# Layer 0 of the style convolutions: the second tap's high and low data stacked in one matmul

## The reference

```python
def _layer(x, style, w, b, mw, mb, typ):
    s = style @ mw.T + mb
    weight = SCALE * w * s[:, None, :, None]
    demod = lax.rsqrt(jnp.sum(weight * weight, axis=(2, 3)) + EPS)
    weight = weight * demod[:, :, None, None]
    ...
# TYPES = ('same', 'upsample', 'same', 'downsample')
x = x + _L0_ffn_ref(_L0_cond_ref(x, cond_512, ...), ...)
# _L0_ffn_ref: cw = top-4 weights of sigmoid(x @ gate_w.T) + bias
#   out = sum_e (silu(x @ Wg[e].T) * (x @ Wu[e].T) * cw[:, e]) @ Wd[e].T
#   out += silu(x @ Sg.T) * (x @ Su.T) @ Sd.T
```

## Time and profile before

| | us |
|---|---|
| three runs, median | 1182.87 |
| three runs, lowest and highest | 1182.38, 1185.62 |
| profiled execution, its own time | 1183.04 |
| its span (first to last instruction) | 1181.3 |
| PE busy | 1121.3 |
| DVE busy | 797.0 |
| ACT busy | 516.6 |
| POOL busy | 539.8 |

### The profile page before, as it was taken

The page is one execution under the profiler, slowest core; times in us unless marked ns, Lnnn a source line. Parts: engine busy times, 40 slices in busy tenths (PEclk is TensorE's granted clock), DMA queues, the critical chain, the costliest instruction groups (busy, mean ns, idle before and its releaser), DMA issues. The chain is left out here.

```text
span 1181.3 us, 24581 instructions
## 1 busy us (share of the span) xinstructions
PE 1121.3 (95%) x7149; PEld 1006.2 (85%) x7150; DVE 797.0 (67%) x2043; ACT 516.6 (44%) x1245; POOL 539.8 (46%) x639
## 2 busy tenths in 40 slices
PE   4999999999999977979999999999999999999995
PEld 2788888888888866769999999999998899999995
DVE  7788887888888875745655656556567565555653
ACT  4776666666666663122322323223234232222321
POOL 1000131323222364555656565665655566656663
PEclk7999999999999987989999999999999999999998
DMA  7855666666556542267676666766676676665664
GB/s 240 205 144 152 150 151 154 157 154 152 143 143 161 143 100 54 77 176 161 128 149 119 155 118 112 162 114 156 125 160 152 150 174 113 114 112 109 116 115 71
DMA packets 140254, 163.64 MB, mean 139 GB/s; under 512 B 31456, under 2 KB 97088, under 8 KB 138688
## 3 DMA queue, kind: packets, MB, share of 16 engines
q0 software_dynamic: 36000, 75.39, 34.0%
q1 hardware_dynamic: 103888, 87.58, 27.6%
q10 hardware_dynamic: 336, 0.32, 0.1%
HBM read 74.58 MB, written 55.18 MB: 110 GB/s over the span
## 5 line engine op out<-in xcount | busy, mean ns | idle before, releaser
L437 POOL DMA_INDIRECT lists<-entry,place x128 | 127.2, 994 | 347.6 <-DVE x_lo L778 285.8
L1426 PE MATMUL bank<-xt_hi,wup_hi 128*128 128x256 f32 x1104 | 278.2, 284 | 2.0 <-ACT xt_hi L694 1.5
L1426 PE MATMUL bank<-xt_hi,wup_lo 128*128 128x256 f32 x1104 | 278.0, 284 | 0.0
L493 POOL DMA_INDIRECT out_rows<-placed,sid x140 | 227.2, 1623 | 92.4 <-DVE placed L1153 69.2
L581 ACT ACTIVATE t<-bank,cB,cA 128x256 f32<-128x256 f32 (+1 forms) x384 | 176.6, 536 | 102.4 <-PE bank L230 96.7
L1426 PEld LDWEIGHTS bank<-xt_hi,wup_hi 128*128 128x128 f32 x1104 | 212.4, 192 | 6.6 <-issue 2.1
L1426 PEld LDWEIGHTS bank<-xt_hi,wup_lo 128*128 128x128 f32 x1104 | 212.7, 193 | 2.4
L478 POOL DMA_INDIRECT placed<-h_rows,gid x140 | 141.6, 1012 | 119.0 <-PE bank L1404 80.3
L1430 PE MATMUL bank<-xt_lo,wup_hi 128*128 128x256 f32 x1104 | 178.0, 284 | 0.0
L711 ACT ACTIVATE zt_hi<-z 128x256 fp32r<-128x256 f32 x138 | 57.6, 417 | 228.9 <-DVE z L1143 228.9
L1153 DVE TENSOR_SCALAR placed<-bank,all_lists 128x512 f32<-128x512 f32 x138 | 99.6, 748 | 83.4 <-DMA out_rows<-placed,sid 46.1
(11 more groups left out here) (258 smaller groups left out, 2085.4 us busy)
## 6 DMA issues: line engine op xcount, KB each, us to landing
x<-x1p SPq DMA_DIRECT2D x64, 384.0 KB
wraw<-in_Wup SPq DMA_DIRECT2D x11, 1024.0 KB, 7.6
xraw<-in_xq SPq DMA_DIRECT2D x32, 260.0 KB, 2.8
xbase<-in_x SPq DMA_DIRECT2D x32, 256.0 KB, 2.8
h_rows<-hrow SPq DMA_DIRECT2D x128, 64.0 KB
x<-x1p SPq DMA_DIRECT2D x64, 127.0 KB
out_rows<-orow SPq DMA_DIRECT2D x30, 256.0 KB, 2.0
wdraw<-in_Wdn SPq DMA_DIRECT2D x11, 512.0 KB, 10.1
```

What stands on the lines that cost most here:

```text
L437: pool.indirect_dma_start(out=lists, out_offset=bass.IndirectOffsetOnAxis(ap=place[:, home, r, k:k + 1], axis=0), in_=entry[:, home, r, k, ...
L493: pool.indirect_dma_start(out=out, out_offset=bass.IndirectOffsetOnAxis(ap=sid[:, u:u + 1], axis=0), in_=yb[:, u, :], in_offset=None, comp ...
L1426: pe.matmul(dst, lhs[a], rhs[0], start=k == 0 and a == 0, stop=False)
```

## The change

Layer 0's second tap reads only 64 partitions, those of q = 0 and q = 1. The change makes a new tile x0n in which the high part of these 64 partitions stands on partitions 0 to 63 and the low part on 64 to 127, put there by two DMAs (`stack_next`), and repeats the entries of these 64 rows on the other 64 in the second tap's matrix. One matmul with the high weights then does high by high and high by low of that tap; one with 64 rows does low by high. Block 0 still does all six matmuls, its second tap on 64 partitions. For the others there are five, and the last waits for both copies.

```diff
+        x0n = sb("x0n", [P, NB, VP], F32R)
...
+            def stack_next(g):
+                sp.wait_ge(S["x0_hi"], g + 1)
+                sp.wait_ge(S["x0_lo"], g + 1)
+                for a in range(2):
+                    sp.dma_start(x0n[a * (P // 2):(a + 1) * (P // 2)].rearrange("p b v -> p (b v)").bitcast(F32),
+                                 x0[a][0:P // 2].rearrange("p b v -> p (b v)").bitcast(F32)).then_inc(S["x0_stacked"], 16)
+
             stack(0)
             sp.wait_ge(S["x0_hi"], 1)
             sp.wait_ge(S["x0_lo"], 1)
             sp.dma_start(xraw[:, 0], xq[2]).then_inc(S["x_loaded0"], 16)
+            stack_next(1)
...
                     sp.dma_start(xraw[:, 1 - odd], xq[bass.ds(g + 3, 1)].rearrange("a p b v -> p (a b) v")).then_inc(S[f"x_loaded{1 - odd}"], 16)
+                if within(g, 0, G - 2):
+                    stack_next(g + 2)
...
-                same = [columns(FIRST + m, P, lambda a: x0[a][:, :, m:m + V]) for m in range(2)]
+                here = columns(FIRST, P, lambda a: x0[a][:, :, 0:V])
+                following = columns(FIRST + 1, P // 2, lambda a: x0[a][0:P // 2, :, 1:V + 1])
                 pe.wait_ge(S["x0_hi"], g + 1)
-                hi_passes(pe, dst, same)
-                pe.wait_ge(S["x0_lo"], g + 1)
-                lo_passes(pe, dst, same).then_inc(S["l0_done"], 1)
+                if isinstance(g, int) and g == 0:
+                    hi_passes(pe, dst, [here, following])
+                    pe.wait_ge(S["x0_lo"], g + 1)
+                    lo_passes(pe, dst, [here, following]).then_inc(S["l0_done"], 1)
+                else:
+                    hi_passes(pe, dst, [here])
+                    pe.matmul(dst, following[0][1], following[1][0], start=False, stop=False)
+                    pe.wait_ge(S["x0_lo"], g + 1)
+                    lo_passes(pe, dst, [here], last=False)
+                    pe.wait_ge(S["x0_stacked"], g * 32)
+                    pe.matmul(dst, cwt[0][:, FIRST + 1, :], x0n[:, :, 1:V + 1], start=False, stop=True).then_inc(S["l0_done"], 1)
...
-    placed = [place(turned[0], lambda q, j: j + Q * m - q) for m in range(2)]
+    placed = [place(turned[0], lambda q, j: j - q), place(turned[0], lambda q, j: j % (Q // 2) + Q - q)]
```

More of the change, by code:

```diff
@@ L202, in mk_adaln_ffn @@
                  "raw_loaded w_hi w_lo fill_written "
-                 "x_loaded0 x_loaded1  base_loaded0 base_loaded1 x0_hi x0_lo "
+                 "x_loaded0 x_loaded1  base_loaded0 base_loaded1 x0_hi x0_lo x0_stacked "
                  "l0_done l1_done l2_done l3_done t1_ready t2_ready t3_ready h_ready "
```

## The result

The changed kernel takes 1192.85 us, median of five runs (1191.26 to 1197.84), against 1182.87 of the kernel before in five runs on the same chip (1179.85 to 1185.62). The ratio is 1.009, with a 95% interval from 1.007 to 1.0111: slower by 10 us. The forecast was 1189.3 in a range of 1183 to 1198.

A forecast was written before the change was run, and what follows sets the result against it. The prediction took TensorE, busy 95% of the span, as the bound. Start 7.6 us lost, steady loop 2.4 gained and late blocks 1.1 lost made 6.3 lost on 1183.04: 1189.3 us, range 1183 to 1198.

The forecast's parts named there:

- The start: Blocks 0 to 3: copies land late, each layer 0 waits through SP's queue; 7.6 us lost, 5.5 to 10.
- The three ends of layer 0: Layer 0 of blocks 1, 2 and 3 ends at 28.9, 40.2 and 53.7, delays of 1.9, 4.2 and 6.8 us.
- The second step: From layer 0's end in block 1 to that in block 2: 11.3 us where it was 8.96, landing 1.8 to 2.6.
- the clock: After some 4.7 us idle before 53, TensorE's clock may fall for 3 us: 1.5 us lost, half of it counted.
- The removed matmul: One 128x512 matmul of six fewer from the second layer 0 on: 31 at 0.235 us, at most 7.3 us gained.
- The 64-row matmul: Layer 0's second tap: no difference from a 128-row matmul; upper bound 0.08 us on the way in and again out.
- mostly hidden: Any extra cost of the 64-row matmul in layer 0 is mostly hidden, since it stands ahead of a wait.
- The mark set in the prediction: Layer 0's five matmuls starting more than 0.3 us apart around the 64-row one would show its price was wrong.
- The landing of the copies: Steady loop: copies land at 213.2 (212.7 to 213.6), period 13.8; 2.4 us gained over 26 periods.
- the rival built on it: Slow copies: landing at 213.5 to 213.6 each block, plain periods 14.1 to 14.2, 1194 to 1199 us; chance 0.25.
- if above 14, too early: Sign for the steady loop: periods above 14 would mean the copies' landing was sized too early.
- The late blocks: Period from 408.85: 13.3 to 14.0 us where it was 12.49, 1.1 us lost; nothing counted for those behind it.

The follow-up runs named there:

- six_wait: Kernel before plus tile x0n, both copies and TensorE's wait for them, still six 128-row matmuls that do not read the copies: 1188.39 us against 1182.02.
- full_rows_from4: Changed kernel with the 64-row matmul zero-padded to 128 rows, and blocks 0 to 3 on six matmuls without copies: 1180.37 us against 1182.02 of the kernel before.
- ahead_from4: full_rows_from4 with SP issuing the two copies ahead of xraw instead of behind it: 1175.97 us against 1183.29 of the kernel before.
- six_one64: Kernel before, six matmuls and no copies, with only the second tap's low weights by high data matmul on 64 rows: 1190.86 us against 1182.02.
- from4: Changed kernel, 64-row matmul kept, with blocks 0 to 3 on six matmuls and without copies: 1189.08 us against 1183.29 of the kernel before.
- tile_only: Kernel before with only the tile x0n allocated and never used: ratio 0.9941 to the kernel before.
- six_copies: Kernel before plus x0n and two copies of the same size, read from the weights, for which no engine waits: 1179.91 us against 1183.29.

## Why the prediction was right, and where it was not

**Direction and size were right, partly by errors that cancel.** 6.3 us were forecast; the spans show 8.3 and the medians 10.0.

**The start: the right mechanism, the size too small.** "Start in all: 7.6 us lost, 5.5 to 10" was 9.8 (8.26 + 1.53). The three ends of layer 0 were named at 28.9, 40.2 and 53.7; they are 30.2, 41.6 and 55.2. So the steps between them, 11.3 and 13.5 in the prediction, were right to 0.1 (11.4 and 13.6), and the error of the delay lies in the first end. There x_lo was ready 0.6 us later than in the kernel before (26.42 against 25.81), ahead of any copy, and the copy landed 2.4 us after issue (26.99 to 29.38) where 1.8 was taken. The second step came out right by two errors: SP's first stack DMA was earlier by 0.7 and the landing took 3.6 us where 1.8 to 2.6 stood. The other term that was undersized is the clock: it did fall after the 4.16 us of idle, and I had counted half of it, 0.75. The first period is 1.31 longer than a plain one of the same kernel. six_wait has this loss with the wait alone, full_rows_from4 gets rid of it.

**The removed matmul: right.** With x0n allocated and on 128 rows throughout, six matmuls take 13.92 a block and five take 13.68: 0.24 for the 0.235 of the working.

**The 64-row matmul: the step that failed.** "I take no difference from a 128-row one", with an upper bound of 0.16 a block. It costs 0.37 to 0.41 us: 14.23 against 13.86 with nothing else changed, 14.08 against 13.67 the other way. Over 26 periods that is some 10 us, more than the removed matmul brings. With it the steady period adds up: 13.86, 0.06 for the tile, 0.24 less for the matmul and 0.41 for the rows give 14.09, and 14.08 is measured. The bound failed because the row it came from is a first matmul after a pause, and so can't hold what it costs to interrupt a full stream; the trace shows that cost in the loads that are not made ahead, at the change to 64 rows and at the change back. That TensorE has to empty itself in between is the reading that fits; no row shows the inside of the engine. And "mostly hidden, because the matmul stands ahead of a wait" failed with it, since there is no wait in the steady block. The Trainium skill (TensorEngine Tiling (Array Packing), Key Properties) has the rule that a change of tiling mode drains the engine; the trace agrees with it, with steps of 0.33 and 0.43 us around the 64-row matmul in place of 0.23. The mark set in the prediction, five matmuls more than 0.3 us apart around the 64-row one, is met.

**The landing of the copies: about right, by two errors.** Counted from the transposes of the block before (199.78 before, 198.91 after), I had the landing at 13.42. It comes at 209.39 + 2.7 = 212.1 by the median, 13.2 (3.0 in the block shown, 13.5). They are issued 0.4 us earlier than I thought (208.83, or 9.92 behind the transposes, against 10.32), as SP's four stack DMAs take 2.79 in place of 3.29, and they move more slowly than I thought. I had taken xraw's 300 GB/s; alone in the queue, in ahead_from4, they run at 180 to 222. The Trainium skill (SBUF — State Buffer, Door 1: The DMA port swizzle) gives a ceiling of about 218 GB/s for a transfer from partitions 0 to 63, and the trace agrees but for one slice of 222. The rule's rate was right and the rival built on it (plain periods of 14.1 to 14.2) was not: the periods are 14.08, yet with hardly a wait for the copies in them, so the agreement of that number is chance. The sign "if above 14, too early" misled in the same way: the period is above 14, and the landing was sized well. Where the 64-row price is gone, the late copies are real: the 25 periods take 349.03 us in full_rows_from4, and 344.12 in ahead_from4 with the copies ahead of xraw.

**The late blocks: the one step right, the sum not.** The period that starts the late blocks is 13.83 (425.55 to 439.38), in the 13.3 to 14.0 of the prediction, where it was 12.49, and it holds a wait of 2.71 us for the copies. The next one holds another, of 1.48, for which I had counted nothing. But the last five periods together are 4 us shorter. Before and after, from the tables of windows, each over its own five periods:

```profile
408.85:474.80 65.95, 52.46 (x250) 43.84 (x249) 44.01 (x180) 33.22 (x82) 34.30 (x34) 0.84 0.34 79
```

```profile
425.55:487.44 61.89, 48.58 (x249) 39.16 (x247) 44.08 (x180) 33.19 (x82) 32.95 (x33) 0.92 0.36 93
```

PE does the same work in 3.9 us less, at a granted clock of 0.92 against 0.84. In the other kernels the five periods go with the clock in the same way: 65.7 us at 0.84 in six_one64, 61.8 at 0.89 in full_rows_from4, 59.8 at 0.97 in six_wait. Whether this change brings the higher clock about, or it differs from one execution to the next, no run settles; from4, with the same copies, has 64.2 at 0.84.

**The second part: not in the prediction at all.** It is 4.5 us shorter, each side read from one execution, where the five executions of the kernel before differ by 5.8. tile_only shows that an unused tile makes the kernel faster; between the kernels with and without it the second part differs by 2.3 us in the mean. The other 2 lie within what the seven kernels with the tile differ by among themselves. Without these two stretches the change would have cost some 17 us, beyond the range.

## What to carry to other kernels

A matmul on fewer rows was not cheaper here than a full one, and one between full ones cost more than the whole matmul that was saved (0.37 to 0.41 us against 0.235). In such a stream pad the contraction with zeros instead of narrowing it, or put all narrow ones together. When an edit lets a queue that nobody waited for release the bottleneck engine, work out its first rounds apart from its steady state, leave it out where the pipeline is still filling, and issue what is waited for ahead of what is not. Before an edit of some tenths of a per cent is judged, run the kernel with its new tile allocated and nothing else.

## What the runs showed that was not expected

- The price of a change of rows is paid per change and not per matmul: one 64-row matmul or three in a row make the plain period 14.23 or 14.22 in place of 13.86.
- Allocating one tile moves times all over the kernel: list matmuls from 284 to 281 ns, the mean of `wdn_hi,zt_hi` from 412 to 418, SP's four stack DMAs from 3.3 to 2.8 us. Why the addresses matter was not tried.
- SP's issue of the same four stack DMAs took 2.8 us in the steady loop and 4.14 while the weights moved (from4), and 6.41 at the same place in six_copies. That the busy DMA engines delay it is likely, and not tried apart.
- In ahead_from4 the copies from one half of the partitions, SBUF to SBUF, ran at 180 to 222 GB/s, a load of 260 KB into all partitions just behind them at up to 416.
